# Two message-passing layers on one core: the relational layer's edge tiles regrouped into blocks of four gathered by TensorE and eight gathered by GpSimd

## The reference

```python
x = _layernorm(x + sage_two_layers(x, src), axis=-1)
# relational layer, feature = x (512 x 128), weight (3, 128, 128), norm = edge_weight
hr = jnp.einsum('ni,rio->rno', feature, weight)
msg = hr[rel_type, src] * norm[:, None]
h = jax.ops.segment_sum(msg, dst, num_segments=feature.shape[0])
x = _layernorm(x + relu(h), axis=-1)
```

## Time and profile before

| | us |
|---|---|
| Median of 3 runs | 499.74 (499.65 to 503.99) |
| Profiled execution, its own time | 500.82 |
| Its span in the profile | 499.0 |
| PE busy | 478.7 (96%) |
| DVE busy | 390.0 (78%) |
| POOL busy | 332.7 (67%) |
| ACT busy | 310.2 (62%) |

### The profile page before, as it was taken

How to read it: one execution, slowest core, us unless ns; L and a number is a source line. 1 busy time by engine, 2 the same in 40 slices (tenths; PEclk the granted TensorE clock), 3 DMA queues, 4 the chain that set the end, 5 groups by cost and what they waited for, 6 DMA issues and landing times.

```text
span 499.0 us, 13983 instructions
## 1 busy us (share of the span) xinstructions
PE 478.7 (96%) x5078; PEld 375.1 (75%) x5078; DVE 390.0 (78%) x1114; ACT 310.2 (62%) x820; POOL 332.7 (67%) x345
## 2 busy tenths in 40 slices
PE   7999999899999999999999999999999999999994
PEld 1888888788888868888988988888676555555552
DVE  4778887848888865488888588888789898888975
ACT  2458887748888873488888588888643333343331
POOL 1477777777777705777777777775047777777771
PEclk8999999999999999999999999999999999999998
DMA  6667767797777706777777777766022222112221
GB/s 220 205 185 203 205 197 207 206 299 208 206 202 199 205 21 196 208 208 205 199 204 198 208 202 203 205 198 180 0 91 56 53 51 53 49 53 53 53 53 33
DMA packets 29107, 77.07 MB, mean 154 GB/s; under 512 B 6477, under 2 KB 10006, under 8 KB 29082
## 3 DMA queue, kind: packets, MB, share of 16 engines
q0 software_dynamic: 22272, 69.23, 49.3%
q1 hardware_dynamic: 6392, 7.11, 4.4%
q10 hardware_dynamic: 418, 0.40, 0.2%
HBM read 73.55 MB, written 3.15 MB: 154 GB/s over the span
## 4 chain that ended last, share of the span: by engine, by line
PE 68%; DVE 13%; DMA 6%; ACT 6%; issue 4%; POOL 1%; DVEq 0%; ACTq 0%; SPq 0%
PE gates L792 26%; PE gates L783 16%; PE gates L914 6%; PE gates L810 6%; DMA edge_rows<-msg_table,msg_index 5%; PE work L924 3%; PE work L927 3%; PE gates L750 3%; DVE prod_ig L625 2%; DVE prod_fc L623 2%; DVE h_full L582 2%; ACT msg_hi L484 2%; ACT act_if L413 2%; ACT h_hi L409 1%; POOL edge_rows L382 1%
## 5 line engine op out<-in xcount | busy, mean ns | idle before, releaser
L370 POOL DMA_INDIRECT rows<-gate_table,src_steps x240 | 238.3, 993 | 105.1 <-issue 72.5
L792 PE MATMUL gates<-h_hi,whh_hi 128*128 128x256 f16 x512 | 126.3, 274 | 0.0
L382 POOL DMA_INDIRECT edge_rows<-msg_table,msg_index x96 | 93.0, 968 | 49.6 <-DMA msg_table<-table_sb 20.6
L792 PE MATMUL gates<-h_hi,whh_lo 128*128 128x256 f16 x512 | 125.7, 273 | 0.0
L783 PE MATMUL gates<-ident_scaled,rows 128*128 128x128 f16 x1920 | 118.1, 219 | 3.4 <-issue 3.4
L783 PEld LDWEIGHTS gates<-ident_scaled,rows 128*128 128x128 f16 x1920 | 112.3, 98 | 5.7 <-issue 4.2
L792 PE MATMUL gates<-h_lo,whh_hi 128*128 128x256 f16 x512 | 98.4, 274 | 0.0
L413 ACT ACTIVATE act_if<-gates 128x512 f32<-128x512 f32 x132 | 77.9, 590 | 30.9 <-PE gates L792 25.1
L587 DVE TENSOR_TENSOR h_lo<-h_full,h_hi 128x256 f16<-128x256 f32 x130 | 55.4, 426 | 40.3 <-ACT h_hi L409 30.9
L409 ACT ACTIVATE h_hi<-h_full 128x256 f16<-128x256 f32 x130 | 54.2, 417 | 49.1 <-DVE h_full L582 49.1
L484 ACT ACTIVATE msg_hi<-edge_rows,norm_edges 128x128 f16<-128x128 f32 x96 | 38.2, 401 | 69.4 <-DMA edge_rows<-msg_table,msg_index 50.6
(11 more groups left out here) (100 smaller groups left out, 590.1 us busy)
## 6 DMA issues: line engine op xcount, KB each, us to landing
rows<-gate_table,src_steps POOLq DMA_INDIRECT x240, 3.8
gate_table<-table_sb SPq DMA_DIRECT2D x8, 256.0 KB, 2.0
edge_rows<-msg_table,msg_index POOLq DMA_INDIRECT x96, 2.5
code<-code_table SPq DMA_DIRECT2D x9, 128.0 KB, 5.4
msg_table<-table_sb SPq DMA_DIRECT2D x4, 192.0 KB, 1.8
whhT<-turned_whh SPq DMA_DIRECT2D x2, 256.0 KB, 5.5
src_direct<-src_by_step SPq DMA_DIRECT2D x2, 256.0 KB, 5.5
wihT<-turned_wih ACTq DMA_DIRECT2D x1, 256.0 KB, 4.1
```

What stands on the lines that cost most here:

```text
L370: pool.indirect_dma_start(rows[:, j * K + k, :, :].rearrange("p a g -> p (a g)"), None, gate_table[l], bass.IndirectOffsetOnAxis(src_steps ...
L382: pool.indirect_dma_start(edge_rows[:, n, :], None, msg_rows, bass.IndirectOffsetOnAxis(msg_index[:, i * NG + n:i * NG + n + 1], axis=0)). ...
L792: mm = pe.matmul(gates[:, h, b, q * HN:(q + 1) * HN], w[:, gate * P:(gate + 1) * P], state[:, h, :], start=False, stop=last and q == 1, sk ...
```

## The change

The order of tiles is now written out as 11 blocks of 12 tiles, 4 gathered by PE and 8 by POOL, so PE gathers 44 tiles and POOL 88. A block has two groups of six tiles (22 groups). The loops over tiles are unrolled on all engines.

- PE gathers the four tiles of block c + 1 before it adds the messages of block c. It adds a group as six `msg_hi` matmuls and then six `msg_lo` matmuls. It waits once for each six.
- ACT scales the six tiles of a group one by one into a float32 buffer `msg_full` (two of them), and then rounds all six at once to `msg_hi` (128x768). DVE makes `msg_lo` with one subtraction of 128x768. There are four groups of slots (`AHEAD`).
- `code_onehot` holds eight tiles, so one DVE instruction compares 128x1024. Three of them lie in each group, among the group's six destination one-hots.
- POOL has two sets of eight row buffers. It starts block c when PE has gathered all blocks before c, and reuses a buffer when ACT has scaled the tile of two blocks ago.
- SP loads `code` in 11 pieces, one at every second step of layer 0 from step 8 on.
- Some SBUF buffers are placed over those that only the LSTM layers use.

```diff
-    BATCH = 4
-    FIRST = BATCH
-    order, seen = [], {"G": 0, "P": 0}
-    for kind in "GGGP" * (2 * BATCH):
-        order.append((kind == "P", seen[kind]))
-        seen[kind] += 1
-    NM, NG, NPE = len(order), seen["G"], seen["P"]
-    ET = TILES // NM
-    PT = ET * NPE + FIRST
-    GT = ET * NG
-    MS = NM // 2
-    GB = NG // 2
+    NPE, NG = 4, 8
+    NM = NPE + NG
+    GR = NM // 2
+    BLOCKS = TILES // NM
+    PT = BLOCKS * NPE
+    GT = BLOCKS * NG
+    BATCH = 2 * NPE
+    AHEAD = 4
...
-        def edge_column(i, m):
-            by_pe, n = order[m]
-            return bass.ds(i * NPE + (FIRST + n) if by_pe else i * NG + (PT + n), 1)
-        def unscaled(by_pe, n):
-            return gate_bank[n % 4][:, 0:C] if by_pe else edge_rows[:, n, :]
+        def tiles_of(c):
+            by_pe, by_pool = [(True, n) for n in range(NPE)], [(False, n) for n in range(NG)]
+            return by_pe + by_pool if c else by_pool + by_pe
+        def edge_column(c, m):
+            by_pe, n = tiles_of(c)[m]
+            column = c * NPE + n if by_pe else PT + c * NG + n
+            return slice(column, column + 1)
+        def gathered(c, n):
+            return gate_bank[2 * (c % 2) + n // 2][:, n % 2 * C:(n % 2 + 1) * C]
+        def groups():
+            return ((k, *divmod(k, 2)) for k in range(2 * BLOCKS))
...
-            sp.wait_ge(h_full_ready[0], T // 2)
-            for t in range(0, PT, BATCH):
-                sp.dma_start(code[:, t * P:(t + BATCH) * P],
-                             code_table[t:t + BATCH, :].rearrange("t p -> (t p)").partition_broadcast(P)
+            for c in range(BLOCKS):
+                sp.wait_ge(h_full_ready[0], T // 4 + 2 * c)
+                sp.dma_start(code[:, c * NPE * P:(c + 1) * NPE * P],
+                             code_table[c * NPE:(c + 1) * NPE, :].rearrange("t p -> (t p)").partition_broadcast(P)
...
-            position = [m for m, (by_pe, _) in enumerate(order) if not by_pe]
-            for i in range(ET):
+            for c in range(BLOCKS):
+                if c >= 1:
+                    pool.wait_ge(pe_gathered, c * NPE)
                 for n in range(NG):
-                    if i > 0:
-                        pool.wait_ge(msg_lo_ready, (i - 1) * NM + FIRST + position[n] + 1)
+                    if c >= 2:
+                        pool.wait_ge(msg_full_ready, (c - 2) * NM + tiles_of(c - 2).index((False, n)) + 1)
                     pool.indirect_dma_start(
-                        edge_rows[:, n, :], None, msg_rows,
-                        bass.IndirectOffsetOnAxis(msg_index[:, i * NG + n:i * NG + n + 1], axis=0)
-                        ).then_inc(edge_rows_in[n], 16)
+                        edge_rows[:, c % 2, n, :], None, msg_rows,
+                        bass.IndirectOffsetOnAxis(msg_index[:, c * NG + n:c * NG + n + 1], axis=0)
+                        ).then_inc(edge_rows_in[c % 2][n], 16)
...
-            def message_hi(slot, column, tile):
-                act.activation(msg_hi[:, slot, :], unscaled(*tile), ACT.Copy,
-                               scale=norm_edges[:, column]).then_inc(msg_hi_ready, 1)
-            for n in range(FIRST):
-                act.wait_ge(pe_gathered, n + 1)
-                message_hi(MS + n, slice(n, n + 1), (True, n))
-            with act.Fori(0, ET) as i:
-                for m, (by_pe, n) in enumerate(order):
+            for k, c, g in groups():
+                if k >= 2:
+                    act.wait_ge(msg_lo_ready, k - 1)
+                for m in range(g * GR, (g + 1) * GR):
+                    by_pe, n = tiles_of(c)[m]
                     if by_pe:
-                        act.wait_ge(pe_gathered, i * NPE + (FIRST + n + 1))
+                        act.wait_ge(pe_gathered, (c + 1) * NPE)
                     else:
-                        act.wait_ge(edge_rows_in[n], i * 16 + 16)
-                    act.wait_ge(msg_free, i * NM + (FIRST + m + 1))
-                    message_hi(m % MS, edge_column(i, m), (by_pe, n))
-            act.wait_ge(msg_free, TILES + MS)
+                        act.wait_ge(edge_rows_in[c % 2][n], 16 * (c // 2 + 1))
+                    act.activation(msg_full[:, k % 2, m - g * GR, :], gathered(c, n) if by_pe else edge_rows[:, c % 2, n, :],
+                                   ACT.Copy, scale=norm_edges[:, edge_column(c, m)]).then_inc(msg_full_ready, 1)
+                if k >= AHEAD:
+                    act.wait_ge(msg_free, k - AHEAD + 1)
+                act.wait_ge(msg_full_ready, (k + 1) * GR)
+                act.activation(msg_hi[:, k % AHEAD, :, :], msg_full[:, k % 2, :, :], ACT.Copy).then_inc(msg_hi_ready, 1)
+            act.wait_ge(msg_free, 2 * BLOCKS)
...
-            def build_code(edges, buffer, b):
-                dve.tensor_scalar(code_onehot[:, buffer, b, :], code[:, edges], block_iota[:, b:b + 1], None,
-                                  op0=ALU.is_equal).then_inc(code_onehot_ready, 1)
+            def build_code(batch, b):
+                first, end = batch * BATCH * P, min((batch + 1) * BATCH, PT) * P
+                dve.tensor_scalar(code_onehot[batch % 2][:, b, 0:end - first], code[:, first:end], block_iota[:, b:b + 1],
+                                  None, op0=ALU.is_equal).then_inc(code_onehot_ready, 1)
...
-            def onehot_of_destination(slot, column):
-                dve.tensor_scalar(dst_onehot[slot], node_iota[:, :], dst_f[:, column], None,
-                                  op0=ALU.is_equal).then_inc(onehot_ready, 1)
-            def message_lo(slot, column, tile):
-                dve.scalar_tensor_tensor(msg_lo[:, slot, :], unscaled(*tile), norm_edges[:, column],
-                                         msg_hi[:, slot, :], op0=ALU.mult, op1=ALU.subtract
-                                         ).then_inc(msg_lo_ready, 1)
-            for n in range(FIRST):
-                onehot_of_destination(MS + n, slice(n, n + 1))
-            for n in range(FIRST):
-                for b in range(n * NB // FIRST, (n + 1) * NB // FIRST):
-                    build_code(slice(BATCH * P, 2 * BATCH * P), 1, b)
-                dve.wait_ge(msg_hi_ready, n + 1)
-                message_lo(MS + n, slice(n, n + 1), (True, n))
-            with dve.Fori(0, ET) as i:
-                for m, tile in enumerate(order):
-                    dve.wait_ge(msg_free, i * NM + (FIRST + m + 1))
-                    onehot_of_destination(m % MS, edge_column(i, m))
-                    dve.wait_ge(msg_hi_ready, i * NM + (FIRST + m + 1))
-                    message_lo(m % MS, edge_column(i, m), tile)
-                    half, b = m // MS, m % MS
-                    if b == 0:
-                        dve.wait_ge(pe_gathered, i * NPE + (half + 1) * BATCH)
-                    if b < NB:
-                        build_code(bass.ds(i * (NPE * P) + (half + 2) * BATCH * P, BATCH * P), half, b)
+            for b in range(NB // 2):
+                build_code(1, b)
+            for k, c, g in groups():
+                if k >= AHEAD:
+                    dve.wait_ge(msg_free, k - AHEAD + 1)
+                for m in range(g * GR, (g + 1) * GR):
+                    dve.tensor_scalar(dst_onehot[c % 2 * NM + m], node_iota[:, :], dst_f[:, edge_column(c, m)], None,
+                                      op0=ALU.is_equal).then_inc(onehot_ready, 1)
+                    batch = (c + 3) // 2
+                    if m % 2 == 0 and batch * BATCH < PT:
+                        if c % 2 == 1 and m == 0:
+                            dve.wait_ge(pe_gathered, (c + 1) * NPE)
+                        build_code(batch, m // 2 + (NB // 2 if c % 2 == 0 else 0))
+                dve.wait_ge(msg_hi_ready, k + 1)
+                dve.tensor_tensor(msg_lo[:, k % AHEAD, :, :], msg_full[:, k % 2, :, :], msg_hi[:, k % AHEAD, :, :],
+                                  ALU.subtract).then_inc(msg_lo_ready, 1)
...
-            pe.sem_inc(msg_free, MS)
             pe.matmul(work[:, 1, :], zeros16[:, 0:P], zeros16[:, :], start=True, stop=False, skip_group_check=True)
             keep_warm(work[:, 0, :], 2 * WARM)
             pe.wait_ge(table2_lo_ready, K)
-            def gather(buffer, n):
-                for b in range(NB):
-                    r, k = divmod(b, K)
-                    for part, table in enumerate((table2_hi, table2_lo)):
-                        mm = pe.matmul(gate_bank[n % 4][:, 0:C],
-                                       code_onehot[:, buffer, b, n % BATCH * P:(n % BATCH + 1) * P],
-                                       table[:, k, r * C:(r + 1) * C], start=(b == 0 and part == 0),
-                                       stop=(b == NB - 1 and part == 1))
-                mm.then_inc(pe_gathered, 1)
-            def add_message(slot, hi_count, lo_count):
-                pe.wait_ge(onehot_ready, hi_count)
-                pe.wait_ge(msg_hi_ready, hi_count)
-                pe.matmul(work[:, 1, :], msg_hi[:, slot, :], dst_onehot[slot], start=False, stop=False,
```

(44 more changed lines are left out.)

45 lines of the change are left out of this document (25 added, 20 removed).

## The result

The changed kernel took 499.25 us (median of 20 runs, 495.77 to 503.32) beside 502.06 us of the kernel before in the same sitting. The ratio is 0.9944, 95% interval 0.9919 to 0.9968, so 2.8 us faster. It was timed again in two later experiments (1.0016 and 0.9973), and the mean of the three is 0.998, about 1 us. The intervals of the first two don't overlap (0.9919 to 0.9968, 0.9993 to 1.0039), so how much the change gives also differs from one sitting to the next, by more than a sitting's own interval. The forecast was 7.4 us less. The profiled execution took 499.08 us.

A forecast was written before the change was run, and what follows sets the result against it. POOL's gathering rate was taken as the bound; eight gathers fewer remove 8.2 us, less 0.8 us allowance leaves 7.4. Profiled 500.82 becomes 493.4, and the median, 1.08 below, 492.3 us; range 489.0 to 498.0.

The forecast's parts named there:

- the allowance in the sum: Relational stage: two chains ending together and DVE's nine one-hots in a row cost 0.01 us per gather, 0.8 us in all.
- the gather at 193.43: Kernel before: a gather inside four one-hots takes 0.95 us, cited as showing POOL gets in between two DVE instructions.
- PE's own work: Relational stage: PE's matmuls grow by 10.7 to 115.8 us; with 2.3 us of start waits PE ends at 483.1.
- The last group: Stage's end: gather 88 starts at 476.9; landing, scaling, rounding, subtraction and adding follow, and PE ends at 483.4.
- DVE's double width: Code one-hots of double width on DVE: 0.40 us each, bounds 0.26 and 0.53.
- POOL's wait for PE: POOL's new wait before each block for PE's gathers: costs nothing, with 6 us of room at block 10.
- Outside the stage: Layer 1's wider one-hots, SP's moved code loads in layer 0 (-0.8 to +0.8) and the removed memset: taken as 0.
- PE pays for every hand-over: Rival: PE, now the bound, loses 0.5 us in ten blocks, 5 us, giving 497.3 us; chance 0.16.
- DVE locks POOL out: Rival: one-hots in a row slow POOL's gathers to a distance of 1.54 us, giving 515 us; chance 0.09.
- my decision point of 1.37: POOL's gather distance in us from which DVE's lock decides; above 1.42 the kernel is slower by over 1%.
- Both chains have less in their way: Rival: no start waits and POOL's last group in time, PE ends at 480.8, giving 488.9 us; chance 0.05.
- these two signs of being wrong: Relational stage: POOL's distance passing 1.37 us, or PE's waits between blocks summing to more than 3 us.

The follow-up runs named there:

- e1: The changed kernel run again without any edit: 501.88 us, ratio 1.0016 to the kernel before.
- e4: The changed kernel with POOL's wait for PE's gathers removed: 500.94 us, ratio 1.0007 to the kernel before.
- e9: The changed kernel unaltered, timed again beside three variants: 500.37 us, ratio 0.9973 to the kernel before.
- e16: The changed kernel unaltered, in the place where the kernel before takes 674 us: 652.64 us, ratio 0.9692.
- e10: The changed kernel with DVE's first run of one-hots delayed until POOL's first row has landed: 499.70 us, ratio 0.9972 to the kernel before.
- e2: The changed kernel with POOL gathering only blocks 0 and 1, later blocks reusing old rows (output not the reference's): 495.94 us, ratio 0.9887 to the kernel before.
- e3: The changed kernel with DVE building only two batches of code one-hots, reused later (output not the reference's): 499.59 us, ratio 0.9946 to the kernel before.
- e17: The changed kernel with DVE's first run late and each destination one-hot made only once ACT scaled its tile: 499.48 us, ratio 0.9947 to the kernel before.

## Why the prediction was wrong

**The sign was right, the size was not**: 2.8 us of 7.4 in the first timing, about 1 us over three. The 499.25 us lie 1.3 above the forecast's range.

The step that failed is the allowance in the sum: "DVE's nine one-hots in a row can hold POOL a little: I give 0.01 us per gather, 0.8 us in all." It measured 0.035 us per gather in the first profile, 3.1 us. There are seven profiles with the wide one-operand run in its old place: after, e1 to e4, e9 and e16. In five of them 2.7 us more came once, at the first gather, and in e16 1.5 us at the second. I had argued from the gather at 193.43, which I took to be inside a row of narrow one-hots at no cost. It isn't: it starts 0.02 us before that row (193.45), so it doesn't show that a gather gets in between two of them. The gather of 1.24, which starts inside a row of seven, I set aside as the rival's evidence, and it was the nearer row.

The other steps:
- *PE's own work*, 115.8 us and 2.3 of start waits: right. The chain has 5.36 and 5.18 per block, and with POOL taken out the stage is, by the estimate above, 118.2 without the late first gather. At the start PE's second group ended 18.4 us after the stage's begin (383.90 + 2.76 - 368.27). Predicted was 18.3: rounded at 380.7, and 12 x 0.215 = 2.6 to add it, less 365.04. What it waited for last was DVE's one-hots, not ACT.
- *The last group*, 6.5 us from gather 88 to PE's end: 6.75 where the clock held (landing 2.49, rounding 0.84 for 0.80, subtraction 0.96 for 0.93). I had no term for the clock: 1.5 to 1.7 us more in three of the eight profiles of changed kernels that gather all 88 tiles with one-operand one-hots.
- *DVE's double width*, taken at 0.40 us between 0.26 and 0.53: 370.65 to 371.04 in the first profile, 0.39. Right in DVE's own time; its price was on POOL.
- *POOL's wait for PE*: nothing, as predicted (e4), where POOL is the bound.
- *Outside the stage*: 0 as far as can be told. From the first one-hot product to the stage it is 351.7 us in the kernel before (365.04 - 13.35) and 351.4 to 352.5 in seven of the nine changed kernels of one-operand form. In the other two (the first profile after, 353.2, and e10, 353.0) the product of about 199 us takes 1.6 longer. In the place of 674 us both kernels have such a long product; in that of 501 there is one profile of the kernel before, without it, so whether the change makes it more frequent is open. The start of the first product has the same gap: 13.60 to 15.64 in the nine, 13.35 in the one.

The stage's lengths fit the medians roughly: 121.7, 127.1 and 125.8 in the three profiles of the changed kernel, 124.9 in the mean, 1.9 below before, where the three timings say 1.1. That the first timing lay nearer to the forecast than the mean is luck of the sitting.

The rivals. "PE pays for every hand-over" gave 497.3, nearest to the time, but for the wrong reason: with POOL taken out, PE has no wait between blocks (e2). "DVE locks POOL out" had the right mechanism and the wrong size, a distance of 1.54, where 1.307 came; it stayed under my decision point of 1.37, which marks where the change stops paying and not where the forecast leaves its range. PE's waits between blocks were 0.4 us, so neither of these two signs of being wrong came. "Both chains have less in their way" needed gathers at under 1.25 us, and no kernel of the table has them. The Trainium skill's lock ("SBUF — State Buffer", section "SBUF: two separate sides"), which I had weighed there, gave the right direction, but for one instruction; the held first gathers wait for the whole run.

**Open**: in which executions a gather at the start is held (one was in six of seven profiles, and no unprofiled run shows it); what of DVE's one-operand one-hots lengthens the gathers after it, as neither their width and number (e3) nor the length of their rows (e17) explains it; why the late first run, with a stage 4 us shorter, gained 0.7 us in the median; what makes the places of 501 and of 674 to 690 us, why PE pauses in the second, and why the change is worth 3% there.

## What to carry to other kernels

Work taken off the bound engine is worth its rate only if that rate stays. Before pricing the freed part, ask whether the new order puts longer or denser work on the engine that can hold the bound one, and price that from the worst row, not from the one that came off free. To see who is the bound after a change that makes two chains end together, take one of them out. An edit that spreads work by waits must be counted in the trace, row by row, before it is said to have failed to spread or failed to help. And a row that is taken as proof that two engines don't meet must start inside the other's run, not just before it.
